# A recommendation tower on one core: gathered rows transposed by VectorE, one joint table, 64-column tiles, a split last layer, and a new order of steps

## The reference

```python
e = jnp.stack([tbl_0[ids[:, 0]], ..., tbl_39[ids[:, 39]]], axis=1)   # (2048, 40, 32)
z = jnp.einsum('bke,kef,bkf->bk', e[:, I], W, e[:, J])               # W: (780, 32, 32)
h = jnp.concatenate([z, dense_ctx], axis=1)                          # (2048, 796)
h = jnp.maximum(h @ W_top1 + b_top1, 0.0)                            # 512 wide
h = jnp.maximum(h @ W_top2 + b_top2, 0.0)                            # 256 wide
y = h @ W_top3                                                       # (2048, 1)
```

## Time and profile before

| | |
|---|---|
| time, median of 3 runs | 684.99 us (684.2 to 687.2) |
| the profiled execution: its time, its span | 685.17 us, 683.6 us |
| PE busy | 660.2 us, 97% of the span |
| DVE busy | 522.0 us, 76% |
| POOL busy | 433.1 us, 63% |
| ACT busy | 232.9 us, 34% |
| mean DMA rate | 47 GB/s |

### The profile page before, as it was taken

The page is one execution under the profiler, slowest core; times in us unless marked ns, Lnnn a source line. Parts: engine busy times, 40 slices in busy tenths (PEclk is TensorE's granted clock), DMA queues, the critical chain, the costliest instruction groups (busy, mean ns, idle before and its releaser), DMA issues.

```text
span 683.6 us, 13973 instructions
## 1 busy us (share of the span) xinstructions
PE 660.2 (97%) x5920; PEld 192.6 (28%) x5920; DVE 522.0 (76%) x483; ACT 232.9 (34%) x200; POOL 433.1 (63%) x452
## 2 busy tenths in 40 slices
PE   5679999999999999999999999999999999999998
PEld 1222323222322333222332233322222222222232
DVE  5687889999967668778987887568978778688900
ACT  6636675164554338630164313501010110010002
POOL 6777777777777777777777777777777774000000
PEclk9999999999999999999999999999999999999999
DMA  7832022111221021111222102001022210000000
GB/s 261 299 87 60 14 75 75 18 26 29 78 62 30 14 60 33 41 29 30 45 52 57 45 14 45 13 15 30 14 57 50 46 29 9 16 17 0 3 3 1
DMA packets 26454, 32.22 MB, mean 47 GB/s; under 512 B 10436, under 2 KB 18372, under 8 KB 26136
## 3 DMA queue, kind: packets, MB, share of 16 engines
q1 hardware_dynamic: 11736, 23.41, 11.1%
q0 software_dynamic: 14336, 7.37, 7.1%
q10 hardware_dynamic: 320, 0.56, 0.3%
HBM read 20.75 MB, written 0.06 MB: 30 GB/s over the span
## 4 chain that ended last, share of the span: by engine, by line
PE 94%; ACT 3%; DVE 1%; issue 1%; DMA 1%; ACTq 0%; DVEq 0%
PE t_ps L637 30%; PE z_ps L667 27%; PE x_ps L686 11%; PE x_ps L597 9%; PE t_ps L686 4%; PE t_ps L645 3%; PE x_ps L699 3%; PE x_ps L613 2%; PE t_ps L597 2%; ACT one_hot L460 1%; ACT one_hot L463 1%; PE x_ps L710 1%; PE t_ps L699 1%; DMA z_sb<-hot_tables 1%; DVE prod L555 0%
## 5 line engine op out<-in xcount | busy, mean ns | idle before, releaser
L555 DVE TENSOR_TENSOR prod<-t_ps,e_t 128x1024 f32<-128x1024 f32 x400 | 466.8, 1218 | 107.8 <-PE t_ps L637 76.1
L415 POOL DMA_INDIRECT rows<-tbl,idx x448 | 432.9, 966 | 139.9 <-issue 135.9
L637 PE MATMUL t_ps<-e_t,w_sb 32*128 32x512 f32 x1440 | 219.8, 640 | 1.1 <-DVE prod L555 1.0
L667 PE MATMUL z_ps<-prod,select 128*32 128x512 f32 x1600 | 207.8, 600 | 2.3 <-DVE prod L555 1.8
L637 PEld LDWEIGHTS t_ps<-e_t,w_sb 32*128 32x128 f32 x1440 | 65.9, 182 | 140.1 <-DVE prod L555 75.0
L460 ACT ACTIVATE one_hot<-hot_sb,row_number 128x2048 bf16<-128x2048 f16 (+1 forms) x44 | 85.4, 1940 | 36.6 <-PE x_ps L597 34.7
L686 PE MATMUL x_ps<-z_sb,w_sb 128*32 128x512 f32 x672 | 83.4, 597 | 0.7 <-ACT e_t L472 0.7
L463 ACT ACTIVATE one_hot<-one_hot 128x2048 bf16<-128x2048 bf16 (+1 forms) x44 | 81.5, 1853 | 1.4
L597 PE MATMUL x_ps<-one_hot,tables 128*32 128x512 bf16 x1074 | 72.7, 387 | 1.7 <-DVE tables L521 1.0
L667 PEld LDWEIGHTS z_ps<-prod,select 128*32 128x32 f32 x1600 | 39.3, 108 | 122.1 <-issue 61.6
L497 ACT COPY z_sb<-z_ps 128x512 f32<-128x512 f32 x28 | 16.4, 586 | 159.3 <-PE z_ps L667 159.2
(11 more groups left out here) (27 smaller groups left out, 83.8 us busy)
## 6 DMA issues: line engine op xcount, KB each, us to landing
rows<-tbl,idx POOLq DMA_INDIRECT x448, 2.3
hot_sb<-hot_ids SPq DMA_DIRECT2D x10, 512.0 KB
e_t<-e_t SPq DMA_DIRECT2D x80, 64.0 KB
...
```

Source lines behind the costliest of these rows:

```text
L415: pool.indirect_dma_start(out=rows[:, slot, t, E * f:E * f + E], out_offset=None, in_=tables[PER * c + f], in_offset=bass.IndirectOffsetOn ...
L555: nc.vector.tensor_tensor(prod[:, u % PROD_SLOTS, :, :], t_ps[:, at:at + 2, :], by, ALU.mult).then_inc(mult_done, 1)
L637: mm = nc.tensor.matmul(t_ps[:, at + r % 2, :], w_sb[part, b, :], e_t[part, e_slot(k, g), :], start=True, stop=True)
L667: mm = nc.tensor.matmul(z_ps[E * q:E * q + E, :], select[:, E - PER - PER * s:2 * E - PER - PER * s], prod[:, u % PROD_SLOTS, q % 2, :], s ...
```

## The change

1. **Rows transposed in blocks.** POOL now gathers a group so that 32 partitions belong to each field: partition 32f + b of `rows` holds, in 16 blocks, the rows of examples b, 32 + b, and so on. One DVE instruction transposes all 32x32 blocks of the slot straight into `e_t`. PE's transposes, ACT's copy and the identity matrix go.
2. **One joint table.** The 28 gathered tables are one DRAM tensor. DVE adds each field's first row to the indices once at the start, and POOL waits for that. It is still 16 indirect DMAs of 128 rows for a group.
3. **64-column tiles** for every gen: two matmuls of 64 columns where there was one of 128.
4. **Last layer in column tiles**: four matmuls of 128 examples beside each other where there was one of 512, for each of the two steps. ACT copies 128x128 where it copied 1x512.
5. **Last chunk's layer 1 begun early**: for its first 5 banks of z (20 steps) the sums go to `x_ps` and are copied by ACT to `h1_sb`; the last 8 steps go to `t_ps`; DVE adds the two and ACT applies ReLU.
6. **A new `ORDER`.** It has the same steps, with 59 one-hots on ACT where it had 44, and 53 on DVE where it had 68.

The names `SUMMED` and `JOINED` in the new code belong to a list that is empty; nothing is done for them.

```diff
+EARLY = 5
+SUMMED = []
...
-    layer1 += [("layer1", chunks - 1, m, kb) for kb in range(Z_BANKS) for m in range(H1_TILES)]
+    layer1 += [("layer1", chunks - 1, m, kb) for m in range(H1_TILES) for kb in range(EARLY)]
+    layer1 += [("layer1", chunks - 1, m, kb) for kb in range(EARLY, Z_BANKS) for m in range(H1_TILES)]
...
-        "r": [("red", n) for n in range(chunks * BATCHES)],
-        "t": [("turn", k, c) for k in range(chunks) for c in GATHERED],
+        "r": [("red", k, b) for k in range(chunks) for b in REDUCED],
+        "t": [("turn", k, c) for k in range(chunks) for c in range(HOT[k], GROUPS)],
...
-        rows = sb("rows", [P, ROW_SLOTS, TILES, P])
+        rows = sb("rows", [P, ROW_SLOTS, SPANS, E])
...
         def _(pool):
-            pool.wait_ge(idx_loaded, 16)
-            for n, (k, c) in enumerate(items):
+            pool.wait_ge(idx_made, 1)
+            for n in range(len(items)):
                 slot = n % ROW_SLOTS
                 if n >= ROW_SLOTS:
-                    pool.wait_ge(x_made, use_no["e", *items[n - ROW_SLOTS]] + 1)
-                for t in range(TILES):
-                    for f in range(PER):
-                        pool.indirect_dma_start(
-                            out=rows[:, slot, t, E * f:E * f + E], out_offset=None,
-                            in_=tables[PER * c + f],
...
+                    pool.wait_ge(turned, n - ROW_SLOTS + 1)
+                for span in range(SPANS):
+                    pool.indirect_dma_start(
+                        out=rows[:, slot, span, :], out_offset=None, in_=table,
+                        in_offset=bass.IndirectOffsetOnAxis(ap=idx[:, n, span:span + 1], axis=0),
+                    ).then_inc(gathered[slot], 16)
...
+                    if use[0] == "h1 early":
+                        nc.scalar.copy(h1_sb[:, m, :], bank_of(use)).then_inc(x_taken, 1)
+                    else:
+                        into = bank_of(use)
+                        if k == chunks - 1:
+                            act.wait_ge(h1_joined, m + 1)
+                            into = h1_sb[:, m, :]
...
-                    nc.scalar.copy(y_sb[:, :], x_ps[0:1, :]).then_inc(x_taken, 1)
+                    nc.scalar.copy(y_sb[:, :], x_ps[:, 0:P]).then_inc(x_taken, 1)
...
+            nc.vector.tensor_tensor(idx[:, :, :], idx_raw[:, :, :], first_row.unsqueeze(2).broadcast_to(idx.shape),
+                                    ALU.add).then_inc(idx_made, 1)
...
+                elif kind == "turn":
+                    c = step[2]
+                    n = item_no[k, c]
+                    dve.wait_ge(gathered[n % ROW_SLOTS], (n // ROW_SLOTS + 1) * GATHER)
+                    wait_for_place(dve, k, c)
+                    nc.vector.transpose(e_t[:, e_slot(k, c), :],
+                                        rows[:, n % ROW_SLOTS, :, :].rearrange("p s e -> p (s e)")).then_inc(turned, 1)
...
+                elif kind == "layer1" and k == chunks - 1 and step[3] == Z_BANKS - 1:
...
+                    nc.vector.tensor_tensor(h1_sb[:, m, :], t_ps[:, tail_banks["h1", k, m], :], h1_sb[:, m, :],
+                                            ALU.add).then_inc(h1_joined, 1)
...
-            def turn(step):
...
-                for t in range(TILES):
-                    mm = nc.tensor.transpose(x_ps[:, t * P:(t + 1) * P], rows[:, slot, t, :], ident[:, :])
-                mm.then_inc(x_made, 1)
...
-                    if g < c:
-                        mm = nc.tensor.matmul(t_ps[:, at + r % 2, :], w_sb[part, b, :], e_t[part, e_slot(k, g), :],
+                    near = far = e_slot(k, g)
+                    if g == c:
+                        near, far = e_slot(k, c + r // 2), fold_slot(k, c + r // 2)
+                    for side in range(2):
+
+                        source = far if (r, side) in ((1, 0), (3, 1)) else near
+                        cols = slice(P // 2 * side, P // 2 * side + P // 2)
+                        mm = nc.tensor.matmul(t_ps[cols, at + r % 2, :], w_sb[part, b, cols], e_t[part, source, :],
                                               start=True, stop=True)
...
-                mm = nc.tensor.matmul(x_ps[0:1, :], w3_sb[:, j:j + 1], h2_sb[:, j, :], start=first, stop=ends)
+                for q in range(PER):
+                    mm = nc.tensor.matmul(x_ps[E * q:E * q + 1, 0:P], w3_sb[:, j:j + 1], h2_sb[:, j, P * q:P * q + P],
+                                          start=first, stop=ends)
```

Of the `ORDER` string the last line shows the end of the last chunk (the first is before, the second after):

```diff
-r3grgrgrgrgrgr3grgrg11rr111111111111111111111111121222222233
+1grrg1rg1rg11g1r11g11r11g1rgr1rg11rg11grr11r1111112222222233
```

More of the change, by code:

```diff
@@ L24 @@
 HOT_GROUPS = 3
-GATHERED = list(range(HOT_GROUPS, GROUPS))
+HOT = [3, 3, 3, 3]
 TABLE_PARTS = 3
@@ L50 @@
 ROW_SLOTS = 8
+SPAN = P // PER
+SPANS = NB // SPAN
 H1_TILES = 4
 H2_TILES = 2
-DENSE_AT = PER * (BATCHES - (Z_BANKS - 1) * Z_SLOTS)
+CHUNKS = 4
+EARLY = 5
+SMALL = Z_BANKS - 2
+SMALL_SLOTS = BATCHES - (Z_BANKS - 1) * Z_SLOTS
+SUMMED = []
+REDUCED = [b for b in range(len(BURSTS)) if b not in SUMMED]
+JOINED = SMALL - 1
+DENSE_AT = PER * SMALL_SLOTS
 INNER = [{0: [(0, 1), (0, 2), (0, 3)], 1: [(1, 2), (1, 3), (2, 3)]},
@@ L143, in steps_of @@
             at[letter] += 1
+    for below, above in (("layer1", "layer2"), ("layer2", "layer3")):
+        for k in range(chunks - 1):
+            read = max(n for n, step in enumerate(steps) if step[:2] == (above, k))
+            assert read < min(n for n, step in enumerate(steps) if step[:2] == (below, k + 1) and use_of(step)[2])
     assert at["o"] == len(lookups) and all(at[letter] == len(kind) for letter, kind in kinds.items())
@@ L150, in use_of @@
     kind, k = step[:2]
-    if kind == "turn":
-        return ("e", k, step[2]), True, True
     if kind == "hot":
@@ L173, in tower_kernel @@
     all_blocks = sum(blocks)
[L174 removed]
+    assert M1 == H1_TILES and M2 == H2_TILES and chunks == CHUNKS
     steps = steps_of(chunks, blocks)
@@ L465, in _ @@
                     act.wait_ge(x_made, use_no[use] + 1)
-                if kind in ("turn", "hot") and ends:
+                if kind == "hot" and ends:
                     c = step[2]
-                    if item(k, c) >= E_RING:
-                        before = divmod(item(k, c) - E_RING, GROUPS)
-                        act.wait_ge(mult_done, last_unit_with(*before) + 1)
+                    wait_for_place(act, k, c)
                     nc.scalar.copy(e_t[:, e_slot(k, c), :], bank_of(use)).then_inc(x_taken, 1)
@@ L715, in _ @@
                 kind = step[0]
-                if kind in ("turn", "red") and not any(s[0] in ("turn", "red") for s in steps[:n]):
-                    pe.wait_ge(selects_loaded, 2 * 16)
+                if kind == "red" and not any(s[0] == "red" for s in steps[:n]):
+                    pe.wait_ge(selects_loaded, 16)
                 if kind == "ids":
@@ L721, in _ @@
                     look_up(step)
-                elif kind == "turn":
-                    turn(step)
                 elif kind == "gen":
@@ L726, in _ @@
                 elif kind == "red":
-                    red(step[1])
+                    red(step[1], step[2])
                 elif kind == "layer1":
@@ L793 @@
     ids_all = np.asarray(inputs["ids"])[:, order]
-    idx_lay = ids_all.reshape(-1, P, FIELDS).transpose(1, 0, 2)
+    cold = order[PER * min(HOT):]
+    first_row = np.cumsum([0] + [table_rows[f] for f in cold])[:-1].reshape(-1, PER)
+    ids_k = ids_all.reshape(-1, SPANS, SPAN, GROUPS, PER)
+    items = [(k, c) for k in range(ids_k.shape[0]) for c in range(HOT[k], GROUPS)]
+    idx_lay = np.stack([ids_k[k, :, :, c, :].transpose(2, 1, 0).reshape(P, SPANS) for k, c in items], axis=1)
+    assert sum(table_rows) < 2 ** 24
     hot_tables = np.zeros((P, sum(blocks), PER, E), np.asarray(inputs["tbl_0"]).dtype)
@@ L803 @@
     row_numbers = (np.arange(max(blocks))[None, :] * P + np.arange(P)[:, None]).astype(np.float32)
-    tables = [None if f in hot else give(f"tbl_{f}", inputs[f"tbl_{f}"]) for f in order]
+    row_numbers = np.concatenate([row_numbers] + [np.repeat(first_row[c - min(HOT)], SPAN)[:, None].astype(np.float32)
+                                                  for _, c in items], axis=1)
+    table = give("cold_tables", np.concatenate([np.asarray(inputs[f"tbl_{f}"]) for f in cold]))
     args = [
```

206 lines of the change are left out of this document (133 added, 73 removed).

## The result

| | before | changed |
|---|---|---|
| time, median | 685.34 us (684.2 to 687.2, 4 runs) | 651.59 us (650.7 to 651.82, 4 runs) |
| span of the profiled execution | 683.6 us | 649.9 us |

The ratio is 0.950 (95% interval 0.948 to 0.953). The forecast was 657.0 in 649 to 667; the time is 5.4 us under it. The other eight ran later, while the kernel before itself took 1177 to 1189 us; their times are set only against each other and against that number.

A forecast was written before the change was run, and what follows sets the result against it. PE's own work was taken as the bound, busy 97% of the span. Span 683.6 - 26.1 (steps) - 0.3 (y copy) - 2 (waits) = 655.2 us, so a time of 657, range 649 to 667 for 8 in 10.

The forecast's parts named there:

- PE's steps: On PE: turns 16.5, layer 3 5.1, 64 columns 4.9 us off, shape changes 0.4 added; 26.1 us less, to 608.
- rival of column tiles that don't overlap: Layer 3 and 64-column gens on PE: 0.05 us of load shows on each of 400 passes, 677 us; chance 0.03.
- The y copy: Copy of y at the end, 0.57 us for 1x512: 128 columns can save up to 0.4, taken as 0.3.
- Waits up to the 41st gen: First part of PE's span: stays tied to DVE, its 29 us of waits stay, 41st gen starts near 157.
- the new order also saves waits at the start: Before the first gen: 2 ACT one-hots ahead for 3, saving 6 us, so 650 us; rival's chance 0.12.
- Waits after it: PE's waits after the 41st gen: 13 us kept, less 2 us gained by the early layer 1.
- As before: DVE after the 41st gen: about 396 of 480 us, 82%, against 80% before, so the 13 us of waits are kept.
- DVE is late more often: Transposes of 1.22 us add 15 us to DVE; 40 more gens meet a late half, 671 us; rival's chance 0.07.
- POOL: POOL's gathers against the turns that need them: slack 22 us at the last turn, 4 us in chunk 0.
- would wait for POOL, as the rival has it: POOL sets the pace and is slower: a late gather in DVE's queue stops all products; chance 0.03.
- 598 / 448: Last turn due at 598 us over 448 gathers: POOL begins to matter at 1.32 us a gather.
- ACT waited for: Between gen 20 and 40, 12 ACT one-hots for 4; four more waits of 2 us, 665 us; rival's chance 0.13.

The follow-up runs named there:

- The other eight: Changed kernel with 128-column gens (three runs), whole layer 3 (two), transposes made twice, a 17th gather per group, or 208 gathers for 448; 834.07 to 1226.92 us.
- ids_first: Changed kernel with ACT making the half-precision copy of the indices at the first ids step, not the second; 644.01 us, ratio 0.940.
- no_early: Changed kernel without the early layer 1: EARLY is 0 and the 20 steps stand behind the last gen; 657.4 us, ratio 0.959.
- new_code_old_order: Changed kernel with the old ORDER, early layer 1 off, two turns moved ahead by one and two letters; 672.29 us, ratio 0.981.
- gathers_17: Changed kernel with a 17th indirect DMA of 128 rows per group into an unread spare tile; 1226.92 us, ratio 1.032.
- old_code_new_order: Kernel before with the new ORDER, 16 of 28 turns moved by up to 25 letters, last chunk's layer 1 behind the last gens; 719.01 us, ratio 1.050.

## Why the prediction was right, and where it was off

- **PE's steps** (the sum 16.5 + 5.1 + 4.9 - 0.4): counted 26.1 us, from 634.4 to 608.3. The single prices hold: a transpose on DVE 0.701 us, a gen alone 1.044, a layer-3 step 0.22. The rival of column tiles that don't overlap is out. The Trainium skill, "TensorE: Matmul & The Clock Gate", section "The mechanism" of Part 3, lets a weight load overlap with matmuls in flight only when its row group differs. The trace goes against that here: four column tiles on the same rows, each with its own load, take 0.108 us a pass, and a gen in two halves 1.044. The same section also lets a load go ahead into the background weight buffer, which I had left out of my reading.
- **The y copy**: forecast to save up to 0.4, 0.3 taken; it is 265 ns against 0.57. Right.
- **Waits up to the 41st gen** ("stay tied to DVE, 29 us"): 30.1, right in sum but not in make. The waits for ACT one-hots of the earlier trace rows mostly went (4.0 and 2.0 us before, now 1.59 and 1.13), as the rival "the new order also saves waits at the start" had it, and the hole of 7.6 us took their place. Neither the prediction nor a rival had this: I followed the one-hots in the new order and not the copy that SP's queue hangs on. Had I, some 5 us could be read, by which the broadcast is issued later; ids_first shows that the hole costs 7.6. Without it these waits are 22.4 us, 6.9 fewer than before. So two misses of some 7 us with opposite signs left the sum within 1.1 us of the forecast, and that is luck.
- **Waits after it** ("13 us less the 2"): the term that was mis-sized. They were 3.9 for 11; less 1.1 us more in the first part and a start 0.3 later, that is the distance to the forecast. The early layer 1 is worth 5.8 us in place of 2 (no_early; its waits after the 41st gen are 9.6). I had taken the 2.4 us that the last 20 gens of the kernel before wait. The new code without the early steps waits more than that there: in no_early the gens behind 550 us stand some 6 us longer than at 1.04 each, in the changed kernel half a us. As I read it PE has less to do between the products there, with no turns and shorter gens, and without the early steps the stretch is gens and reds alone. The other 3 us of the 8.8 come with the order in the middle (12.7 before, 9.6 in no_early, and 23.8 in new_code_old_order): from 200 to 450 us the changed kernel has hardly a wait (some 0.6 us).
- **The order** was the largest thing that I costed at nothing. "As before" was taken for DVE's share of 82%; that its share is the same doesn't say that its work lies where PE can cover it. With the old order the new code waits 55.4 us in all; with the new order and layer 1 at the end, as there, 41.0 (no_early), and 7.6 of these are the hole. The time between these two is 14.9 us. So the forecast of the waits held only because the new order takes back what the new code adds. I hadn't worked that out, so this too was luck. The rival "DVE is late more often" is true of the new code with the old order, and not of the changed kernel.
- **POOL**: never waited for, as said. The last transpose starts at 594.25, and its last gather starts at 569.66 and takes 0.94: so some 22 us were left, as forecast. In chunk 0 it was 7.6 to 9.1 us for its last four groups with 4 forecast, because of the hole: in ids_first, without it, two transposes wait 0.57 and 0.52 us for their gathers. A kernel much faster than that one would wait for POOL, as the rival has it. Does a transpose hold POOL? By the profile gathers that overlap a transpose by over 0.1 us and no one-hot take 944 ns in the mean (28 of them), like those that overlap neither, and those that overlap a DVE one-hot 1064 ns (54). So a DVE instruction that locks GpSimd out of the port pair, as the Trainium skill, "SBUF — State Buffer", section "SBUF: two separate sides", has it, may be what slows the gathers beside one-hots; for this transpose the trace shows nothing of it. Whether POOL at 17 gathers a group would be late isn't known, since gathers_17 ran only beside a kernel before of 1186 us. The prediction's 598 / 448 is 1.33 and not 1.32, unless the start of the gathers is taken off; nothing rests on it.
- **ACT waited for**: no; ACT has 269.4 us, and PE waits for a one-hot of ACT 2.7 us in all.

Left open: the changed kernel's own time with wide gens or the whole layer 3 (only their steps are measured), what of the 34 us that old_code_new_order lost goes to the late copies, and the cause of the 1.7 times.
